# Perceiver stack on one core: stage 11's dispatch, residual and output in parts, negated maxima on ScalarE, wide exponentials in stage 9's tail

## What is computed

```
x = x + _L0_xattn_ref(...)               # stage 0: one head, masked, 4096 keys
x = x + _L1_xattn_ref(...)               # stage 3: one head, no mask
x = x + _L2_xattn_ref(...)               # stage 6: one head, no mask
x = x + _L3_xattn_ref(...)               # stage 9: 16 heads of 16, masked, 4096 keys
x = x + _L3_ffn_ref(_layernorm(x), ...)  # stage 11
```

## Time and profile before

| | us |
|---|---|
| median of 3 runs | 1437.22 (1436.2 to 1438.24) |
| the profiled execution, its own time | 1435.54 |
| its span, first to last instruction | 1433.8 |
| PE busy | 1376.1 (96%) |
| DVE busy | 953.4 (66%) |
| ACT busy | 805.6 (56%) |
| POOL busy | 370.4 (26%) |

### The profile page before, as it was taken

The page is one execution under the profiler, slowest core; times in us unless marked ns, Lnnn a source line. Parts: engine busy times, 40 slices in busy tenths (PEclk is TensorE's granted clock), DMA queues, the critical chain, the costliest instruction groups (busy, mean ns, idle before and its releaser), DMA issues.

```text
span 1433.8 us, 24150 instructions
## 1 busy us (share of the span) xinstructions
PE 1376.1 (96%) x9532; PEld 973.4 (68%) x9541; DVE 953.4 (66%) x1559; ACT 805.6 (56%) x1481; POOL 370.4 (26%) x485
## 2 busy tenths in 40 slices
PE   7999999999999999999999989999999998999897
PEld 4897668886998676998567645555555554645686
DVE  5676744335786576786366578889999973566533
ACT  5774344344665555664555437778888884325232
POOL 3986332002642204542101332222121200100100
PEclk9999999999999999999999989999999999999999
DMA  9413342234214513212316255353535404210140
GB/s 372 156 56 132 129 171 81 89 95 166 97 60 152 194 60 126 97 60 76 130 72 272 76 198 167 121 183 123 194 129 183 152 2 189 89 59 2 59 177 15
DMA packets 49072, 177.77 MB, mean 124 GB/s; under 512 B 4864, under 2 KB 6144, under 8 KB 43008
## 3 DMA queue, kind: packets, MB, share of 16 engines
q1 hardware_dynamic: 48960, 176.23, 34.3%
HBM read 132.66 MB, written 44.60 MB: 124 GB/s over the span
## 4 chain that ended last, share of the span: by engine, by line
PE 74%; DVE 7%; ACT 3%; issue 1%; POOL 0%; ACTq 0%; DVEq 0%
PE PS L160 44%; PE PS L2387 9%; PE PS L2291 7%; PE PS L2305 4%; PE PS L630 2%; DVE SM L2402 2%; PE PS L1877 1%; PE PS L1898 1%; PE PS L2378 1%; PE PS L1905 1%; PE PS L2875 1%; PE PS L266 1%; DVE CNr L3094 0%; PE PS L1635 0%; ACT L283 0%
## 5 line engine op out<-in xcount | busy, mean ns | idle before, releaser
L2402 DVE TENSOR_REDUCE SM<-PS 128x1 f32<-128x1024 f32 x256 | 310.6, 1223 | 34.4 <-PE PS L2291 31.1
L160 PE MATMUL PS<-ARr 128*128 128x256 f32 (+1 forms) x1024 | 269.9, 335 | 0.5 <-POOL CNr L931 0.5
L160 PE MATMUL PS<-CNr,ARr 128*128 128x256 f32 (+1 forms) x952 | 199.1, 316 | 4.0 <-DVE ARr L792 3.7
L160 PEld LDWEIGHTS PS<-ARr 128*128 128x128 f32 x1024 | 179.9, 189 | 18.6 <-issue 0.8
L160 PEld LDWEIGHTS PS<-CNr,ARr 128*128 128x128 f32 x952 | 151.4, 190 | 18.6 <-DVE ARr L792 5.1
L160 PE MATMUL PS<-ARr,HTr 128*128 128x512 f32 x384 | 121.0, 396 | 0.5 <-ACT CN L459 0.5
L2291 PE MATMUL PS<-ARr 64*128 64x512 f32 x320 | 118.9, 454 | 0.7 <-DVE SM L2402 0.4
L2305 PE MATMUL PS<-ARr 64*128 64x256 f32 x640 | 116.5, 304 | 0.8 <-DVE ARr L2418 0.5
L853 ACT CAST ARr<-PS 128x512 fp32r<-128x512 f32 x96 | 56.2, 585 | 90.3 <-PE PS L630 90.1
L2470 ACT ACTIVATE AR<-PS 128x512 f32<-128x512 f32 x172 | 93.4, 605 | 16.8 <-PE PS L2305 13.4
L931 POOL TENSOR_TENSOR CNr<-CN,ARr 128x256 fp32r<-128x256 f32 x120 | 83.2, 728 | 72.0 <-ACT ARr L848 72.0
(11 more groups left out here) (412 smaller groups left out, 2756.0 us busy)
## 6 DMA issues: line engine op xcount, KB each, us to landing
CT<-k_tiles SPq DMA_DIRECT2D x64, 512.0 KB, 5.0
CN<-ctx_n SPq DMA_DIRECT2D x24, 1024.0 KB, 5.2
k_tiles<-CNr SPq DMA_DIRECT2D x32, 768.0 KB, 3.5
CT<-pack SPq DMA_DIRECT2D x6, 2048.0 KB, 8.1
v_ones<-CN SPq DMA_DIRECT2D x30, 288.0 KB, 2.8
CT<-ctx_t SPq DMA_DIRECT2D x8, 1024.0 KB, 19.1
k_tiles<-CN SPq DMA_DIRECT2D x32, 256.0 KB, 4.0
AR<-pack SPq DMA_DIRECT2D x16, 512.0 KB, 3.4
```

What stands on the lines that cost most here:

```text
L160: last = te.matmul(o, l, r, start=first and k == 0, stop=final and k == n - 1, skip_group_check=True)
L2402: ve.tensor_reduce(MX9[:, p % 2, e, g % 2, g % 8 // 2:g % 8 // 2 + 1], PS[:, b:b + 2, :].rearrange("p a b -> p (a b)"), AX, ALU.max).then_inc(
```

## The change

(1) In stages 0, 3 and 6 ScalarE makes nb, from mx and ahead of al; VectorE no longer does. (2) In the last ten groups of stage 9 the scores of a step take a pair of banks, LR9 has three pairs, and one exponential of 1024 stands for two of 512. (3) In each dispatch of stage 11 VectorE fills D11 in the order of row tiles, and TensorE takes a row tile as soon as both experts' part of it is there; 6 instead of 8 unread matmuls stand ahead of the first. (4) DB11 of expert 0 is made ahead of the hidden products. (5) GpSimd adds X2 to X behind H11R, and VectorE's end is one instruction for a half. (6) The last combine signals after two row tiles, and X leaves in two transfers.

```diff
@@ -752,13 +752,6 @@
                             *dv.inc("largest", "mx", s, g))
-                    dv.wait_ge(("mx", s, g))
-                    if masked:
-                        ve.tensor_scalar(of(nb, g), top[:, i, n + 1, 0:1], -1.0, None, ALU.mult).then_inc(
-                            *dv.inc("largest", "nb", s, g))
-                    else:
-                        ve.tensor_tensor(of(nb, g), c, top[:, i, n + 1, 0:1], ALU.subtract).then_inc(
-                            *dv.inc("largest", "nb", s, g))
@@ -854,8 +847,10 @@
                     i, n = tile_of(g), part_of(g)
+                    ac.wait_ge(("mx", s, g))
+                    ae.activation(of(nb, g), top[:, i, n + 1, 0:1], ACT.Identity, scale=-1.0,
+                                  bias=0.0 if masked else of(cadd, i)).then_inc(*ac.inc("exp", "nb", s, g))
                     if n:
-                        ac.wait_ge(("mx", s, g))
@@ -2273,7 +2268,7 @@
 
-        LR9 = banks.ring((0,), (1,), (2,), (3,), (4,), (5,), (6,))
+        LR9 = banks.ring((0, 1), (2, 3), (4, 5))
@@ -2293,8 +2288,7 @@
             def score_bank(p, s, e):
-                ring = SR9 if 8 * p + s // 2 + AHEAD < 128 else LR9
-                b, before = ring.take(("st", 9, p, s, e), ("e", 9, p, s, e))
+                b, before = SR9.take(("st", 9, p, s, e), ("e", 9, p, s, e))
@@ -2316,7 +2310,9 @@
             def both(p, s):
-                ba, bb = score_bank(p, s, 0), score_bank(p, s, 1)
+                ba, before = LR9.take(("st", 9, p, s, 2), ("e", 9, p, s, 0))
+                bb = ba + 1
+                pe.wait_ge(*before, ("mrow", 9, p))
@@ -2471,6 +2467,12 @@
 
+            def exp_both(p, s):
+                i, b = 16 * p + s, banks.of("st", 9, p, s, 2)[0]
+                ac.wait_ge(("st_ps", 9, p, s, 0), ("st_ps", 9, p, s, 1), ("mix", 9, (i - 6) // 16, (i - 6) % 16))
+                ae.activation(PT9[i % 6], PS[:, b:b + 2, :].rearrange("p e (c q) -> p (e c) q", c=2), ACT.Exp).then_inc(
+                    *ac.marks("exp", [("e", 9, p, s, e) for e in range(2)]))
+
@@ -2483,8 +2485,7 @@
                 if what == "both":
-                    exp(n // 8, 2 * (n % 8) + k, 0)
-                    exp(n // 8, 2 * (n % 8) + k, 1)
+                    exp_both(n // 8, 2 * (n % 8) + k)
@@ -2928,12 +2929,15 @@
                     if e == 0:
-                        keep_pe(pe, 8, 11, "dispatch", e)
+                        keep_pe(pe, 6, 11, "dispatch", e)
                     b, before = PB.take(("bt", e), ("bt", e))
-                    pe.wait_ge(*before, ("d", e + 1, 3), *[("h11r", i) for i in range(4)])
-                    for kt in range(2):
-                        z = mm(te, PS[:, b, kt * 256:kt * 256 + 256],
-                               [(h[:, i, tok(kt)], D11[e // 2 % 2][:, i, :]) for i in range(4) for h in (H11H, H11R)])
+                    pe.wait_ge(*before)
+                    for i in range(4):
+                        pe.wait_ge(("d", e + 1, i), ("h11r", i))
+                        for kt in range(2):
+                            for part, h in enumerate((H11H, H11R)):
+                                z = te.matmul(PS[:, b, kt * 256:kt * 256 + 256], h[:, i, tok(kt)], D11[e // 2 % 2][:, i, :],
+                                              start=i == kt == part == 0, stop=i == 3 and part == 1, skip_group_check=True)
@@ -2967,11 +2971,13 @@
                             z = te.matmul(ACC[i], DT11F[:, tok(i)], YG11[p], start=False, stop=True, skip_group_check=True)
+                            if i == 1:
+                                z.then_inc(*pe.inc("expert", "summed", 0))
...
                                               start=e == n == 0 and i % 2 == 0, stop=False, skip_group_check=True)
-                    z.then_inc(*pe.inc("expert", "combined", e))
+                    z.then_inc(*(pe.inc("expert", "summed", 1) if e == 7 else pe.inc("expert", "combined", e)))
@@ -3088,8 +3094,8 @@
                 if what == "dispatch":
-                    for n in (e, e + 1):
-                        for i in range(4):
+                    for i in range(4):
+                        for n in (e, e + 1):
@@ -3148,12 +3154,10 @@
             for q in range(2):
-                xv, x2v = (a[:, 2 * q:2 * q + 2, :].rearrange("p a b -> p (a b)") for a in (X, X2))
-                dv.wait_ge(("combined", 7))
-                ve.scalar_tensor_tensor(out=x2v, in0=PS[:, 6 + q, :], scalar=1.0 - 0.2, in1=x2v, op0=ALU.mult,
-                                        op1=ALU.add).then_inc(*dv.inc("x", "x2_end", q))
-                dv.wait_ge(("x2_end", q))
-                ve.tensor_tensor(xv, xv, x2v, ALU.add).then_inc(*dv.inc("x", "x", 11, q))
+                xv = X[:, 2 * q:2 * q + 2, :].rearrange("p a b -> p (a b)")
+                dv.wait_ge(("summed", q), ("x_x2", 2 * q), ("x_x2", 2 * q + 1))
+                ve.scalar_tensor_tensor(out=xv, in0=PS[:, 6 + q, :], scalar=1.0 - 0.2, in1=xv, op0=ALU.mult,
+                                        op1=ALU.add).then_inc(*dv.inc("x", "x", 11, q))
@@ -3190,7 +3194,7 @@
                             *ac.inc("expert", "bt", e))
-                if what == "gates":
+                if what == "rows" or what == "gates" and e:
@@ -3228,6 +3232,9 @@
                     *pl.inc("split", "h11r", i))
+            for i in range(4):
+                pl.wait_ge(("x2", i))
+                ge.tensor_tensor(X[:, i, :], X[:, i, :], X2[:, i, :], ALU.add).then_inc(*pl.inc("row", "x_x2", i))
@@ -3312,9 +3319,12 @@
             sync_11(sp)
+            rows = out.rearrange("b (i p) d -> p (b i) d", p=128)
+            for q in range(2):
+                sp.wait_ge(("x", 11, q))
+                sp.e.dma_start(rows[:, 2 * q:2 * q + 2, :], X[:, 2 * q:2 * q + 2, :]).then_inc(*sp.lands("out", "out", q))
             after(sp, 12)
-            sp.e.dma_start(out.rearrange("b (i p) d -> p (b i) d", p=128), X[:]).then_inc(*sp.lands("out", "out"))
-            sp.wait_ge(("out",))
+            sp.wait_ge(("out", 0), ("out", 1))
```

## The result

The changed kernel took 1423.15 us (median of 4 runs, 1422.84 to 1425.86) against 1436.71 of the kernel before in the same session: ratio 0.9914, 95% interval 0.9899 to 0.9929. It is faster by 0.86%, and by more than the forecast of 1429.1 with its range down to 1426.3 allows. Its profiled execution took 1425.86 with a span of 1424.1; that is 9.7 us less span than before, not 13.6.

The account below looks back on a forecast made before the run. TensorE holds 74% of the chain, so changes pay where it waits or the chain has left it. Eight terms sum to -8.15 us, taken from the 1437.22 median: forecast 1429.1, range 1426.3 to 1432.3.

Parts of the forecast that it names:

- end, issue and landing: End of the kernel: last transfer issued 2.05 us earlier, called sure, and its landing 0.6 shorter (0.1 to 1.45).
- The holding: Last group of stages 3 and 6: GpSimd holds VectorE until its current instruction ends; removing nb gains 0.7 us each.
- The +0.4 that I gave to the first groups: First group of stages 0, 3 and 6: nb takes 0.30 us on ScalarE in place of 0.16, uncovered.
- Rival E: Middle of stages 0, 3 and 6: exponentials wait for ScalarE's own nb in 42 groups; +5.4 us, 1442.7; chance 0.03.
- rival C: Tail of stage 9: gain only at `finish`, -0.8 us in place of -1.9, total 1430.2; chance 0.12.
- "In the other three ... the whole wait of 0.5 goes.": Stage 11's three later dispatches: TensorE's wait for D11 vanishes, -1.5 us together (-1.2 to -1.5).
- The term of 0.7: Stage 11 router: GpSimd's additions hold four VectorE instructions, so instruction 3077 starts 0.7 us later.
- Rival B: Stage 11 router: VectorE blocked for GpSimd's whole 2.8 us, +2.5 in place of +0.7, total 1430.9; chance 0.08.
- rival F: Stage 11: its parts do nothing, only the end and stage 9's tail gain; -4.5 us, 1432.7; chance 0.02.
- "what the three runs spread by (2.0 us)": Whole time: the run-to-run spread that the forecast range of 1426.3 to 1432.3 us was meant to hold.
- rival D: Clock: a half-speed stretch over dense work costs up to 1.7 us or vanishes; 1430.8 or 1427.4; chance 0.15.

Follow-up runs that it names:

- nb part alone: The kernel before with only nb moved to ScalarE in stages 0, 3 and 6; 1432.3 us (12 runs), ratio 0.999.
- a_again: The changed kernel run once more, unaltered; 1425.92 us (6 runs), ratio 0.9945.
- p1_nb_back: The changed kernel with nb made by VectorE again in stages 0, 3 and 6; 1427.83 us (11 runs), ratio 0.9958.
- the filled waits: Unread matmuls in TensorE's waits ending stages 3 and 6: changed kernel with nb back on VectorE, 1427.63 us; with GpSimd's additions behind D11, 1425.06.

## Why the prediction was wrong

Its mechanisms held, one term of its sum was a third too small (the later dispatches), and the time was missed by more than the sum. Term by term, in us:

| | predicted | measured |
|---|---|---|
| nb on ScalarE | -1.0 | -1.36, twice 0.68 |
| wide exponentials | -1.9 | -1.77 |
| first dispatch, D11 to BT11 | -1.2 | -1.16 (3.91 to 2.75 at full clock) |
| three later dispatches | -1.5 | -2.29 |
| DB11 | -0.6 | -0.54 |
| GpSimd's additions | +0.7 | +0.84 under low clock, +1.30 without |
| end, issue and landing | -2.65 | -2.05 - 0.7 |
| sum | -8.15 | -9.0 |

*nb.* The holding was as read from the earlier trace rows. The +0.4 that I gave to the first groups is there at the first turn and gone behind it: in stages 3 and 6 that turn waits 0.38 and 0.43 where it waited 0.25 and 0.29, but the product behind it then waits 0.60 and 0.53 for its rest instead of 0.78 and 0.74. In stage 3 it is, from the first maximum to the third turn, 359.56 - 350.43 = 9.13 against 361.19 - 352.05 = 9.14. Rival E was never near: to the turn at the end of stage 3 it is 95.50 against 447.56 - 352.05 = 95.51.

*The tail* gained 0.88 at `finish` (predicted 0.8) and 0.9 in the steps (predicted 1.1); rival C, a gain at `finish` alone, is excluded.

*"In the other three ... the whole wait of 0.5 goes."* This step failed in size: each is worth 0.76. The wait in the profile counts from the modelled end of the matmul ahead, but without it the next matmul starts 0.24 before that end. Three times 0.26 is the 0.8 that the sum lacked.

*The router.* Three instructions were held, not four, each to an end of one of GpSimd's. The term of 0.7 was right for the execution it was read from, because the counts were late there by 0.38 anyway; in the profile of the nb part alone, with no low clock over the router, up to 3077 it is 3.59 instead of 4.05, and the additions would have cost the full 1.30. Rival B (2.5) did not come, and rival F falls with every row of the table. By the rule of the Trainium skill that the prediction cites (SBUF — State Buffer, section "SBUF: two separate sides"), a VectorE instruction with two on-chip inputs blocks against a GpSimd one that reads; the trace agrees for the router, where the instructions of 0.80, 0.65 and 0.42 have two and the reductions between them, with one, keep 0.19. The rule names a second kind too, which the prediction left out: VectorE instructions in a mode that uses both ports.

*The step that failed by the most is the range*: "what the three runs spread by (2.0 us)", with rival D, the clock, at one stretch of 1.7 and a chance of 0.15. Single runs of the changed kernel lost 8.5 to 15.7 us to low clock. The miss is 1429.1 - 1423.15 = 5.95. Of it:

- 2.1 is the base. The forecast stands on the median of 3 runs, 1437.22; all 49 runs of the kernel before have 1435.1.
- 0.9 is the terms (9.0 - 8.15).
- 2.15 is luck in the first session of the changed kernel: its four runs have 1423.15, all 16 have 1425.3.
- 0.8 is left between 1435.1 - 9.0 = 1426.1 and 1425.3. With single runs scattered by 1.9 to 2.2 (standard deviation) the medians can't say what it is.

The clock goes the same way as this luck: the profiled execution that the forecast stands on has a mean clock of 0.989, some 15 us lost where 45 runs lost 11.9 on average, and the first four runs of the changed kernel lost 9.9 where 16 lost 12.0. With each run's loss taken off its time, which counts every low stretch as if it lay on dense work, the means are 1422.5 before and 1413.2 after: 9.3 lower, against the 9.0 of the terms.

That the change itself moves the clock is not borne out, as the 11.9 and 12.0 show. The draw shows best where all kernels run the same code, the first product with a weight matrix in stage 0. Of the kernel before:

```profile
10.28 5.37 PE L160 MATMUL PS<-HT,AR 128*128 128x512 f32 x8 [0.51 <-DVE HT L353]
```

Of the changed kernel, first profile and then of the run a_again:

```profile
10.26 3.67 PE L160 MATMUL PS<-HT,AR 128*128 128x512 f32 x8 [0.51 <-DVE HT L353]
```

```profile
10.28 5.37 PE L160 MATMUL PS<-HT,AR 128*128 128x512 f32 x8 [0.51 <-DVE HT L353]
```

The same eight matmuls take 3.67 or 5.37; in p1_nb_back they start at 10.98 and take 5.83, and the next product begins at 17.66 instead of 14.77. So 2.9 us of that profile were lost before the change begins, and its clock row does not show it, so "lost" is too low for such runs. In all 14 profiles the clock is low near 840 us, and in all but that of the nb part alone somewhere between 1326 and 1344. What decides in which runs it is low in the first 16 us, and why other low stretches come at some 350 us in some profiles and at 756 in others, is open; idle TensorE time at the ends of stages 3 and 6 is not it, as far as the filled waits tell.

## What to carry to other kernels

Time a part by the distance between two rows that enclose it, in profiles with and without the part: it repeated to 0.02 us here, where whole times of one kernel spread over 6 to 8 us, and three or four runs gave a median 2 us off. A base of three runs belongs in the range with that spread. A removed wait of TensorE is worth the wait in brackets plus the overlap of matmuls that it had cut off (0.50 and 0.26 here). A small VectorE instruction with two sources beside long ones of GpSimd costs up to one of those (0.61 of 0.69 here, 1.3 for three in a chain), so GpSimd's work belongs where nothing waits for VectorE.

## What the runs showed of the hardware

- A short VectorE instruction beside GpSimd's additions: 0.80, 0.65 and 0.42 us instead of 0.19, each ended within 0.1 of the end of a GpSimd instruction. One instruction with a single tensor source was slower too: at the end of stage 3 of the changed kernel line 764, a TENSOR_SCALAR of 128x256 with its scalar in memory, takes 0.78 from 448.07, beside GpSimd, and 0.35 at 451.36, without; its end, 448.85, is 0.1 behind the end of GpSimd's third (446.59 + 3 x 0.71 = 448.73).
- Two ScalarE instructions of 128x1 in a row start 0.1 to 0.2 apart though each reads 0.30 (nb at 447.43, al at 447.63). From nb to the exponential it is 0.39 with al between them (447.82) and 0.33 without it (351.93 to 352.26 in the first group of stage 3), so al costs 0.06 on the path.
- The transfer of X: 2.9 us for 512 KB in one, 2.2 for each half when there are two.
- In the first 15 us the page's clock row isn't enough: it reads full clock for p1_nb_back from 12 to 16, while the matmuls there take 5.83 us instead of 3.67. That this is the clock is read from the durations alone: in the run a_again the row does read low, and the same matmuls take 5.37.
